# A two-layer decoder kernel: input loads split over two DMA queues, the output projection's weight prepared inside the attention

## What is computed

```python
def quat_linear(x, W, b):              # W (4, 64, 64), b (4, 64)
    xs = x.reshape(B, T, 4, D4)
    A = jnp.einsum('btcd,wdo->btcwo', xs, W) + b
    r = A[:, :, 0, 0] - A[:, :, 1, 1] - A[:, :, 2, 2] - A[:, :, 3, 3]
    i = A[:, :, 1, 0] + A[:, :, 0, 1] + A[:, :, 3, 2] - A[:, :, 2, 3]
    j = A[:, :, 2, 0] - A[:, :, 3, 1] + A[:, :, 0, 2] + A[:, :, 1, 3]
    k = A[:, :, 3, 0] + A[:, :, 2, 1] - A[:, :, 1, 2] + A[:, :, 0, 3]
    return jnp.concatenate([r, i, j, k], axis=-1)
...
q = quat_norm(quat_linear(x, qW, qb)); k = quat_norm(quat_linear(x, kW, kb)); v = quat_linear(x, vW, vb)
scores = jnp.einsum('bthd,bshd->bhts', q_, k_) * scale       # 16 heads of 16
scores = scores + jnp.mean(jnp.sin(J[:T])) * 0.1
attn = jax.nn.softmax(scores, axis=-1)
out = jnp.einsum('bhts,bshd->bthd', attn, v_).reshape(B, T, D)
return quat_linear(out, oW, ob)
```

## Time and profile before

| | |
|---|---|
| median of 3 runs | 887.13 us (886.57 to 887.72) |
| the profiled execution | 884.86 us, its span 883.1 us |
| PE busy | 764.8 us (87%) |
| ACT busy | 553.1 us (63%) |
| DVE busy | 547.7 us (62%) |
| POOL busy | 192.5 us (22%) |
| bytes by DMA | 29.04 MB |

### The profile page before, as it was taken

One profiled execution on the slowest core, in us unless ns is written; L12 is line 12 of the kernel. 1 busy time (PEld: TensorE's weight loads), 2 busy tenths in 40 slices (PEclk: granted clock), 3 DMA queues, 4 the chain that ended last, 5 costly groups with the idle time before them and its releaser, 6 DMA issues.

```text
span 883.1 us, 11318 instructions
## 1 busy us (share of the span) xinstructions
PE 764.8 (87%) x4105; PEld 444.4 (50%) x4105; DVE 547.7 (62%) x1120; ACT 553.1 (63%) x941; POOL 192.5 (22%) x214
## 2 busy tenths in 40 slices
PE   4973999999999989998799998678898979994397
PEld 2641222222222238987688886455665744442286
DVE  4999212121212129779524639869999757898886
ACT  4654899999999971424132142576775533498991
POOL 1768000000000003216003112485453300000012
PEclk9997899999999999999899999899999989998599
DMA  7400000000000300202055000002100000000002
GB/s 219 157 0 1 1 1 1 1 1 2 1 1 2 100 38 1 96 1 96 1 191 190 1 1 1 0 1 72 37 1 0 1 1 0 1 0 0 1 24 72
DMA packets 22719, 29.04 MB, mean 33 GB/s; under 512 B 2979, under 2 KB 20233, under 8 KB 22537
## 3 DMA queue, kind: packets, MB, share of 16 engines
q1 hardware_dynamic: 22520, 28.20, 9.9%
q10 hardware_dynamic: 144, 0.13, 0.1%
HBM read 26.23 MB, written 2.10 MB: 32 GB/s over the span
## 4 chain that ended last, share of the span: by engine, by line
PE 33%; ACT 30%; DVE 27%; issue 7%; POOL 1%; SPq 1%; DMA 1%; DVEq 0%; POOLq 0%; ACTq 0%
ACT arena L509 24%; PE banks L1804 5%; PE banks L1597 5%; PE banks L1796 5%; PE banks L1585 5%; DVE arena L866 2%; DVE arena L874 2%; DVE arena L1098 2%; DVE arena L1105 2%; DVE arena L1177 2%; PE banks L1494 2%; DVE arena L764 1%; PE banks L1697 1%; ACT arena L686 1%; ACT arena L672 1%
## 5 line engine op out<-in xcount | busy, mean ns | idle before, releaser
L509 ACT ACTIVATE arena<-banks 128x1024 f32<-128x1024 f32 x256 | 235.9, 1061 | 10.0 <-PE banks L1344 7.5
L1358 PE MATMUL banks<-arena 128*32 128x512 f32 x1024 | 138.1, 611 | 1.9 <-ACT arena L509 0.8
L333 POOL TENSOR_SCALAR arena<-arena 128x2 f32<-128x2 f32 (+1 forms) x38 | 11.4, 299 | 472.3 <-DVE arena L869 472.3
L1344 PE MATMUL banks<-arena 64*128 64x512 f16 x512 | 89.2, 388 | 12.0 <-ACT arena L509 8.0
L1796 PE MATMUL banks<-arena 128*128 128x512 f32 x192 | 86.0, 610 | 3.8 <-DVE arena L1188 3.7
L600 ACT ACTIVATE arena<-banks,arena 128x77 f32<-128x77 f32 x256 | 58.7, 348 | 36.9 <-DVE arena L1098 36.8
L1344 PEld LDWEIGHTS banks<-arena 64*128 64x128 f16 x512 | 23.0, 93 | 96.0 <-ACT arena L509 78.2
L1804 PE MATMUL banks<-arena 128*128 128x256 f32 x192 | 44.6, 398 | 26.6 <-ACT arena L707 26.6
L1597 PE MATMUL banks<-arena 128*128 128x256 f32 x256 | 58.9, 392 | 5.8 <-DVEq L1004 5.8
L1796 PEld LDWEIGHTS banks<-arena 128*128 128x128 f32 x192 | 37.3, 196 | 51.9 <-issue 48.9
L823 DVE COPY arena<-banks 128x512 f32<-128x512 f32 x16 | 11.1, 691 | 81.4 <-PE banks L1358 81.4
(11 more groups left out here) (221 smaller groups left out, 1408.0 us busy)
## 6 DMA issues: line engine op xcount, KB each, us to landing
arena<-in_L_ffn_w SPq DMA_DIRECT2D x16, 1024.0 KB, 7.4
arena<-in_x SPq DMA_DIRECT2D x4, 512.0 KB, 7.5
out_x<-arena SPq DMA_DIRECT2D x3, 512.0 KB, 2.9
arena<-in_L_ffn_b SPq DMA_DIRECT2D x1, 1024.0 KB, 11.4
arena<-in_L_ffn_w_up SPq DMA_DIRECT2D x1, 768.0 KB, 5.0
arena<-in_L_ffn_w_down SPq DMA_DIRECT2D x1, 768.0 KB, 7.3
arena<-in_L_ffn_w_gate SPq DMA_DIRECT2D x1, 768.0 KB, 4.5
arena<-in_L_xattn_W SPq DMA_DIRECT2D x2, 256.0 KB
```

The lines of the kernel that those rows point to most:

```text
L509: act.activation(PT[kt % 2][:, half], PS[:, 2 * (n % 3):2 * (n % 3) + 2, :], ACT.Exp, scale=DH ** -0.5 / QK_UP ** 2).then_inc(sem("exp_don ...
L1344: mm = pe.matmul(bank(2 * (n % 3) + h), KT[u % 2][64 * h:64 * h + 64, P * kt:P * kt + P], QT[u % 2][64 * h:64 * h + 64, 512 * half:512 * h ...
L1358: mm = pe.matmul(PS[32 * j:32 * j + 32, 6, :], VS[w][:, kt, h, :], PT[kt % 2][:, half, h, :], start=(kt == 0), stop=(kt == TB - 1))
```

## The change

It has three parts.

1. **Loads.** ACT's queue now issues, ahead of `J`, the first two tiles of x, and behind it the q, k and v biases. SP issues only the q, k and v weights ahead of tiles 2 and 3 and the rest of x; the weight and bias of the output projection follow behind x.
2. **Order on ACT and sizes.** The combining of weights and biases covers three maps instead of four. ACT now turns out the first x tile, then builds its weight blocks, and then takes the sine and exponential for `J`, which came first before.
3. **Output projection.** A new DVE function `out_weights`, in unit 0 of the attention, builds the fourth map and its bias: 16 TENSOR_SCALAR and 12 SCALAR_TENSOR_TENSOR. PE waits for it (`quat_wo`) before the output projection, and POOL now waits for it before it adds the bias to x.

```diff
 @block.sync
+            def quat_weight(m, name):
                 for half in range(2):
...
+            for m, w in enumerate(("qW", "kW", "vW")):
+                quat_weight(m, w)
+            sp.dma_start(X[:, 2:4, :], xf[:, 2:4, :]).then_inc(sem("x_in0b"), 16)
+            for g in range(1, G4):
                 sp.dma_start(X[:, 4 * g:4 * g + 4, :], xf[:, 4 * g:4 * g + 4, :]).then_inc(sem(f"x_in{g}"), 16)
...
+            quat_weight(3, "oW")
+            sp.dma_start(braw[:, 3]...ob...).then_inc(sem("quat_wo_in"), 16)
 @block.gpsimd
             pool.wait_ge(sem("x_tr"), T)
+            pool.wait_ge(sem("quat_wo"), 1)
             for g in range(G4):
                 ins = pool.tensor_tensor(X[:, 4 * g:4 * g + 4, :], X[:, 4 * g:4 * g + 4, :],
 @block.scalar
+            act.dma_start(X[:, 0:2, :], xf[:, 0:2, :]).then_inc(sem("x_in0"), 16)
             act.dma_start(Jb, row(a["L0_attn_J"]).to_broadcast([P, D])).then_inc(sem("j_in"), 16)
-            act.wait_ge(sem("j_red"), 1)
-            act.activation(Jk, Jb, ACT.Sin, accum_out=jred).then_inc(sem("j_sin"), 1)
...
-            act.wait_ge(sem("quat_w_in"), 16 * 8)
...
+            for m, b in enumerate(("qb", "kb", "vb")):
+                act.dma_start(braw[:, m]...).then_inc(sem("quat_b_in"), 16)
...
             x_evac(0)
+            act.wait_ge(sem("quat_w_in"), 16 * 6)
+            for c in (1, 3):
+                for o in range(NQ):
+                    ins = act.activation(Wq4[64:128, c // 2, 0:3, DQ * o:DQ * o + DQ], wraw[64:128, 0:3, c ^ o, :], ACT.Copy, scale=sgn(c, o))
+            ins.then_inc(sem("quat_w_upper"), 1)
+            act.wait_ge(sem("j_red"), 1)
+            act.activation(Jk, Jb, ACT.Sin, accum_out=jred).then_inc(sem("j_sin"), 1)
...
 @block.vector
+            def out_weights():
+
+                dve.wait_ge(sem("quat_wo_in"), 16 * 3)
+                for c in range(NQ):
+                    at64 = 64 * (c % 2)
+                    for o in range(NQ):
+                        dve.tensor_scalar(Wq4[at64:at64 + 64, c // 2, 3, DQ * o:DQ * o + DQ], wraw[at64:at64 + 64, 3, c ^ o, :], sgn(c, o), None, ALU.mult)
+                bias(3, 4).then_inc(sem("quat_wo"), 1)
...
                     turned_k(u + 1)
+                if u == 0:
+                    out_weights()
                 dve.wait_ge(sem("pv_done"), TB * u + TB)
                 dve.tensor_copy(OSB[:, u], bank(6)).then_inc(sem("o_evac"), 1)
 @block.tensor
+            pe.wait_ge(sem("quat_wo"), 1)
             out_turn(0)
```

More of the change, by code:

```diff
@@ L259, in _ @@
         def _(sp):
-            for m, w in enumerate(("qW", "kW", "vW", "oW")):
+            def quat_weight(m, name):
                 for half in range(2):
                     sp.dma_start(wraw[64 * half:64 * half + 64, m],
-                                 a["L0_attn_" + w].rearrange("w d o -> d w o")).then_inc(sem("quat_w_in"), 16)
-            for g in range(G4):
+                                 a["L0_attn_" + name].rearrange("w d o -> d w o")).then_inc(sem("quat_w_in" if m < 3 else "quat_wo_in"), 16)
+            for m, w in enumerate(("qW", "kW", "vW")):
+                quat_weight(m, w)
+            sp.dma_start(X[:, 2:4, :], xf[:, 2:4, :]).then_inc(sem("x_in0b"), 16)
+            for g in range(1, G4):
                 sp.dma_start(X[:, 4 * g:4 * g + 4, :], xf[:, 4 * g:4 * g + 4, :]).then_inc(sem(f"x_in{g}"), 16)
[L266 to L269, removed]
+            quat_weight(3, "oW")
+            sp.dma_start(braw[:, 3].rearrange("p w o -> p (w o)"),
+                         row(a["L0_attn_ob"].rearrange("w o -> (w o)")).to_broadcast([P, D])).then_inc(sem("quat_wo_in"), 16)
             sp.wait_ge(sem("ctx_zeroed"), 1)
@@ L445, in _ @@
         def _(act):
+            act.dma_start(X[:, 0:2, :], xf[:, 0:2, :]).then_inc(sem("x_in0"), 16)
             act.dma_start(Jb, row(a["L0_attn_J"]).to_broadcast([P, D])).then_inc(sem("j_in"), 16)
-            act.wait_ge(sem("j_red"), 1)
-            act.activation(Jk, Jb, ACT.Sin, accum_out=jred).then_inc(sem("j_sin"), 1)
-            act.wait_ge(sem("j_sin"), 1)
-            act.activation(ec, jred, ACT.Exp, scale=0.1 / D).then_inc(sem("j_exp"), 1)
-            act.wait_ge(sem("quat_w_in"), 16 * 8)
[L454 to L457, removed]
+            for m, b in enumerate(("qb", "kb", "vb")):
+                act.dma_start(braw[:, m].rearrange("p w o -> p (w o)"),
+                              row(a["L0_attn_" + b].rearrange("w o -> (w o)")).to_broadcast([P, D])).then_inc(sem("quat_b_in"), 16)
             def x_evac(t):
@@ L491, in _ @@
             x_evac(0)
+            act.wait_ge(sem("quat_w_in"), 16 * 6)
[5 more added lines that the diff above has]
+            act.activation(Jk, Jb, ACT.Sin, accum_out=jred).then_inc(sem("j_sin"), 1)
+            act.wait_ge(sem("j_sin"), 1)
+            act.activation(ec, jred, ACT.Exp, scale=0.1 / D).then_inc(sem("j_exp"), 1)
             for t in range(T + 1):
@@ L728, in _, with bias @@
             dve.tensor_scalar(Jb, Jb, 3.1415925, -3.1415925, ALU.min, ALU.max).then_inc(sem("j_red"), 1)
-            dve.wait_ge(sem("quat_w_in"), 16 * 8)
+            dve.wait_ge(sem("quat_w_in"), 16 * 6)
             for c in (0, 2):
                 for o in range(NQ):
-                    ins = dve.tensor_scalar(Wq4[0:64, c // 2, :, DQ * o:DQ * o + DQ], wraw[0:64, :, c ^ o, :], sgn(c, o), None, ALU.mult)
+                    ins = dve.tensor_scalar(Wq4[0:64, c // 2, 0:3, DQ * o:DQ * o + DQ], wraw[0:64, 0:3, c ^ o, :], sgn(c, o), None, ALU.mult)
             ins.then_inc(sem("quat_w"), 1)
[L735 to L742, removed]
-            dve.wait_ge(sem("quat_b"), 1)
+            dve.wait_ge(sem("quat_b_in"), 16 * 3)
+            def bias(m, k):
+                for n, c in enumerate((1, 2, 3)):
+                    for o in range(NQ):
+                        dst = bq4[:, m:k, DQ * o:DQ * o + DQ]
+                        ins = dve.scalar_tensor_tensor(dst, braw[:, m:k, c ^ o, :], sgn(c, o), dst if n else braw[:, m:k, o, :], ALU.mult, ALU.add)
+                    if n < 2:
+                        link(ins)
+                return ins
+            bias(0, 3).then_inc(sem("quat_b"), 1)
+            dve.wait_ge(sem("quat_b"), 1)
+            def out_weights():
+                dve.wait_ge(sem("quat_wo_in"), 16 * 3)
+                for c in range(NQ):
+                    at64 = 64 * (c % 2)
+                    for o in range(NQ):
+                        dve.tensor_scalar(Wq4[at64:at64 + 64, c // 2, 3, DQ * o:DQ * o + DQ], wraw[at64:at64 + 64, 3, c ^ o, :], sgn(c, o), None, ALU.mult)
+                bias(3, 4).then_inc(sem("quat_wo"), 1)
             def mask():
@@ L1295, in x_turn @@
             def x_turn(t):
-                pe.wait_ge(sem(f"x_in{t // 4}"), 16)
+                pe.wait_ge(sem("x_in0b" if t in (2, 3) else f"x_in{t // 4}"), 16)
                 if t >= 2:
```

## The result

| | before | after |
|---|---|---|
| median of 17 runs each, us | 885.69 (882.81 to 887.72) | 888.54 (887.17 to 890.61) |
| profiled execution's span, us | 883.1 | 886.7 |
| mean granted clock of TensorE there | 0.955 | 0.951 |

The ratio after to before is 1.0032, with an interval of [1.0021, 1.0043]: slower by 2.8 us, where a gain of 0.7 was forecast. The time lies inside the range on record (883.0 to 889.4), on the side that had 0.15.

A forecast was written before the change was run, and what follows sets the result against it. Bounds: late start loads, DVE stretched by POOL in the loop's tail, then ACT's back-to-back exponentials. Start 2.7 + tail 6.5 + restart 0.5 - unit 1 9.0 = 0.7 us gained, 887.13 to 886.4 us; range 883.0 to 889.4.

The forecast's parts named there:

- the side that had 0.15: Whole kernel: the outcome slower by over 0.2%, given chance 0.15; faster had 0.35, within 0.2% had 0.50.
- The start: Loads and weight blocks before the projection loop: weight blocks 1.1, tile 0 0.3, PE's idle before tile 2 1.3; 2.7 us gained.
- an allowance for ACT's queue: At the start: vW's expected landing raised from 6.76 to 7.4, since ACT's queue moves 768 KB at the same time.
- the bound above it (9.2): At the start: vW as late as ob's landing, 6.0 us after issue, gives 0.9 gained; as a rival, chance 0.10.
- The ctx, mask and vector loads: At the start: issued about 1.5 us earlier, wanted 2.7 us earlier, PE had not waited for them; cost nothing.
- a shift of tile 3's bias: Projection loop: DVE has no gap worth naming from that bias at 25.47, so shifting it shifts the whole loop.
- The tail: End of projection loop: without POOL's four additions beside it, DVE's stretched instructions shorten to their usual lengths; 6.5 us gained.
- The restart: After the tail: PE, kept busy, could keep a faster clock and save up to 2.0; 0.5 us gained was taken.
- The small instructions: Unit 0: 28 new DVE instructions take 3.8 us inside a 4.51 us gap, so cost nothing by themselves.
- The rival that they outlast it: Unit 0: small instructions cost as much as full-size ones, unit 1 loses 13.1, time 890.5 us; chance 0.10.
- Unit 1: Second attention unit: four staging copies go one for one with POOL's four additions, PE and ACT wait; 9.0 us lost.
- The rival that the copies pass: Unit 1: POOL does not hold up the copies, at most 0.5 us lost, time 877.9 us; chance 0.12.

## Why the prediction was wrong

**The start: the failed step.** The prediction takes 7.4 for the moment from which vW is not waited for, out of 4.78 + 1.98 = 6.76 and an allowance for ACT's queue, and gets 2.7 us gained. Measured: 13.17 in the change, 12.80 and 13.08 in the two runs with only POOL edited. The allowance was the error: it counted bytes (768 KB on ACT's queue), and the bound above it (9.2) took the landing of ob behind three bias loads of its own queue, though vW had three on another queue against it, and x's groups behind it. With ACT's biases away vW was waited for until 6.54; with the same bytes from different rows until 8.24 and 8.56. So, with x's groups behind them, the biases' single row is worth some 4.8 us, the bytes 1.7 to 2.0. The biases were late too: the last landed near 12.3 (2.92 + 9.4), not at 7 to 9. The rest of the step was sound: by its own sum vW at 8.24 and 8.56 gives 1.9 and 1.5 us, and tile 3's bias came at 23.02 and 23.93, 2.45 and 1.54 us ahead of the earlier trace rows.

Two smaller premises failed beside it. The ctx, mask and vector loads were costed at nothing because they would go out 1.5 us earlier; the context rows went out 2.8 us later, and cost nothing only because tile 3 was late as well. With tile 3 at 21.23 PE stood 2.97 us for the mask. And a shift of tile 3's bias does not always shift the whole loop: from there to the staging copies it is 56.5 us with the change, but 57.5 to 58.0 in the run with x's groups held back and in the two with different rows, where DVE waits 0.85 to 1.43 us for PE late in the loop. So 1.0 to 1.5 us of their earlier start are gone by the tail.

The Trainium skill ("Trainium Kernel Development and Optimization", Key Constraints) says that DMAs from all queues share the same 16 engines, and that issuing from several engines saves only issue time. I had it speak for a smaller gain. The runs agree, and show a loss besides: 384 KB on ACT's queue, in different rows, hold SP's vW up by 1.7 to 2.0 us. That the same bytes cost far more when they are one row for all partitions is shown by the run with different rows alone.

How much was lost? By the two profiles 27.56 - 25.47 = 2.1 us. But the start of before comes out early or late, and against the average of its five traces it is 27.52 - 27.08 = 0.4 us. I read the earlier trace rows as what the kernel does and set the whole sum on it, though the text itself says that the median stands 2.3 us above that execution. The two kinds of start can account for that: with a late one the span is 3.2 or 3.7 us longer. That median was of three runs; the one of 17 is 885.69, 0.8 above the execution. So the loss at the start lies between 0.4 and 2.1 us, and the runs do not say where.

**The tail: right.** L784, L795 and L796 take 0.69, 0.42 and 0.69 us as said, without POOL. From tile 3's bias to the staging copies after has 84.06 - 27.56 = 56.50 us, before 88.81 - 25.47 = 63.34: 6.8 us less, for 6.5 forecast. The three later traces of before have 63.3 to 63.4 as well, whatever their start.

**The restart: forecast 0.5 gained, none seen.** From the staging copies to a steady ACT it is 7.00 us in after and 6.60 to 6.80 in four traces of before: 0.3 lost. PE was granted half clock until past 89 us in after. That more could be had shows in the run with the x groups held back: there PE is at full clock from 85 us on.

```profile
86.85 13.89 ACT L515 ACTIVATE arena<-banks 128x1024 f32<-128x1024 f32 x15 [0.27 <-PE banks L1379]
```

ACT is steady 2.75 us after its staging copies (84.10), and at the same exponential it is 2.4 us ahead of after. Its span of 883.8 us, 2.9 less than after's, comes mostly from that and not from its start, whose gain of 0.97 us was gone by the tail. Holding x's groups back need not be the cause: the two traces of the kernel with ordered loads and spread additions, the same program, restart in both ways, steady 2.75 us after the staging copies in one and 6.35 in the other, at a granted clock of 1.00 and of 0.50. So spans of single executions differ by 2 us and more for the clock alone, and the verdicts above rest on medians or on rows within a stage.

**The small instructions: right.** 3.98 us for 3.8 forecast, 0.13 and 0.16 us each, inside the gap. (The 0.11 was nearer to strict proportion than its "two thirds".) The rival that they outlast it is out.

**Unit 1: right.** The four L814 take 8.28 us beside four additions of 2.3, one for one, as the earlier trace rows had it. Eight halves let them pass in 3.99. The rival that the copies pass is out. The loss, forecast 9.0: the seventeenth exponential from the steady point on begins at 115.11 instead of 91.06 + 14.75 = 105.81, so 9.3. The Trainium skill ("SBUF — State Buffer", Who interferes with whom) has a copy in a two-port mode and a GpSimd instruction lock each other out for the whole instruction; 0.62 against 8.28 us agrees with it.

**Sum.** By the two profiles -2.1 + 6.8 - 0.3 - 9.3 = -4.9, the 5.0 us seen at the seventeenth exponential; 1.4 come back behind the attention, which makes the 3.6 between the spans. Against the average start of before it is -0.4 in place of -2.1, so -3.2, or -1.8 with the 1.4. The runs measured -2.8 [-3.8, -1.9], within what the unsure start of before allows. With the 2.7 of the forecast at the start the sum up to the attention's end would be -0.1, "no change": that one term turned it into a loss.

**Left open.** Why one row for all partitions is slow (the source's address, or how the load is cut up) was not tried apart. Nor was why the last bias of before lands anywhere from 14.29 to 15.81. The 1.4 us that the change regains behind the attention, for the most part in the expert products, were not explained. And the two traces of the reordered, spread kernel do not show what makes a restart fast or slow.

## What to carry to other kernels

Move a load to a second queue only after asking what it takes from the loads that gate the first instruction: order all loads by when they are due, whatever queue issues them, and count a row that is spread over all partitions as several times its bytes (here 6.6 us of delay for another load, where different rows cost 1.7 to 2.0). Long GpSimd instructions beside a stage that DVE feeds belong one at a time into gaps, not in a burst at a new place; what a burst costs is about DVE's instruction count in that place times the length of a GpSimd instruction (here four copies beside additions of 2.3 us took 8.28 us). And before building a sum on waits of 1 or 2 us at the start, profile the kernel before more than once: here its first steady point lay anywhere from 25.5 to 28.7 us.

## What the runs showed of the hardware

- Loads of one 1 KB row to 128 partitions hold up others of another queue: 58 to 90 GB/s at a DMA share of 0.53 to 0.78 between 6 and 8 us, and a 64 KB weight half landed 8.97 us after its issue; with different rows 240 GB/s at 1.06.
- A load that landed 0.5 us later cost 2.2 at tile 3's bias: behind an idle time of 1.12 or 1.33 us PE did its next four products in 1.98 us at a granted clock of 1.00, behind one of 2.32 to 2.63 us in 3.35 to 3.68 us, at a granted clock down to 0.50, the lower of its two levels (1.2 of 2.4 GHz). Five traces of one start fell on both sides.
- Half-precision copies of 256 columns, 0.22 us alone, take turns with GpSimd's additions one for one, and shorter additions let more of them through, at the price of 9.86 instead of 9.26 us for all.
